# Thirty-two row scatters in front of 159 adding transfers on one GpSimd queue: eight ahead, the others one behind each of the first 24 adds

## The reference, cut to what matters

```python
tki = jax.lax.top_k(masked, TOPK)[1]                      # 8 of 32 experts for each token
...
combine = (jax.nn.one_hot(tki, E, dtype=tkw.dtype) * tkw[..., None]).sum(1)
g = jax.nn.silu(jnp.einsum('th,eih->tei', h, w_gate))
u = jnp.einsum('th,eih->tei', h, w_up)
routed = jnp.einsum('tei,ehi->th', g * u * combine[:, :, None], w_down)
...
return (routed + shared).reshape(B, S, Hd)
```

## Time and profile before

| | |
|---|---|
| median of 3 runs | 3811.11 us (3809.53 to 3814.87) |
| the profiled execution's own time | 3820.71 us |
| its span, first to last instruction | 3819.0 us |
| busy in the span: PE, DVE, ACT, POOL | 90%, 63%, 47%, 13% |
| stage G | from 3439 us to the end |
| 32 scatters of the last batch on POOL | 3439.1 to 3479.9 us |
| 159 adds on POOL | 3486.9 to 3783.0 us |

### The profile page before, as it was taken

How to read it: one execution, slowest core, us unless ns; L and a number is a source line. 1 busy time by engine, 2 the same in 40 slices (tenths; PEclk the granted TensorE clock), 3 DMA queues, 4 the chain that set the end, 5 groups by cost and what they waited for, 6 DMA issues and landing times.

```text
span 3819.0 us, 62855 instructions
## 1 busy us (share of the span) xinstructions
PE 3441.5 (90%) x21953; PEld 1664.1 (44%) x21953; DVE 2416.8 (63%) x6385; ACT 1804.2 (47%) x3597; POOL 511.0 (13%) x451
## 2 busy tenths in 40 slices
PE   6999989998999889998999899999999889997992
PEld 2352445344352445343452445343452445345881
DVE  5668576755668576854768576853768566853552
ACT  2755534452755434443846434443836434532551
POOL 0000020000001120000002120000002020007885
PEclk9999999999999999999999999999999999998996
DMA  6313001304314101314214101215213201937997
GB/s 215 117 36 69 20 2 49 50 22 152 104 40 94 40 6 49 46 59 148 84 36 91 37 11 48 42 59 174 68 37 84 102 18 47 259 145 170 163 162 171
DMA packets 184290, 317.61 MB, mean 83 GB/s; under 512 B 29972, under 2 KB 139412, under 8 KB 178580
## 3 DMA queue, kind: packets, MB, share of 16 engines
q1 hardware_dynamic: 152888, 270.90, 25.5%
q0 software_dynamic: 29040, 39.86, 5.9%
q10 hardware_dynamic: 2032, 2.61, 0.2%
HBM read 176.94 MB, written 116.70 MB: 77 GB/s over the span
## 4 chain that ended last, share of the span: by engine, by line
PE 70%; DVE 19%; ACT 4%; issue 3%; SPq 1%; DMA 1%; PEldq 1%; another core or an unknown queue 1%; POOL 0%; PEld 0%; POOLq 0%; DVEq 0%; ACTq 0%
PE ps L607 8%; PE ps L590 7%; PE ps L429 5%; DVE mx L773 5%; PE ps L534 4%; PE ps L1865 4%; PE ps L1472 4%; PE ps L1762 3%; PE ps L595 3%; PE ps L1803 3%; PE ps L486 2%; PE ps L1786 2%; DVE ps L770 2%; PE ps L1487 2%; PE ps L638 2%
## 5 line engine op out<-in xcount | busy, mean ns | idle before, releaser
L711 ACT ACTIVATE PT<-ps 128x512 f32<-128x512 f32 (+2 forms) x1280 | 643.9, 564 | 330.3 <-PE ps L595 174.6
L773 DVE TENSOR_REDUCE mx<-ps 128x1 f32<-128x512 f32 (+3 forms) x768 | 431.0, 618 | 84.8 <-PE ps L534 46.0
L590 PE MATMUL ps<-QS,KS 99*128 99x512 bf16 (+2 forms) x1280 | 420.2, 369 | 8.6 <-ACT PT L711 6.9
L534 PE MATMUL ps<-KS,QS 96*128 96x512 bf16 (+3 forms) x1280 | 395.2, 371 | 17.5 <-DVE mx L773 7.1
L770 DVE CUSTOM_DVE_ANT_0 ps<-ps,mneg 128x512 f32<-128x512 f32 x512 | 340.9, 718 | 82.0 <-PE ps L534 78.9
L607 PE MATMUL ps<-PT,VP 128*32 128x512 f32 (+3 forms) x2560 | 375.4, 576 | 0.0
L429 PE MATMUL ps<-mneg,identb 128*128 128x512 bf16 x1240 | 329.1, 394 | 29.3 <-DVE a_fin L1980 10.9
L407 POOL TENSOR_TENSOR rstd<-mv,half 128x4 f32<-128x4 f32 x20 | 20.3, 1015 | 2499.1 <-DVE mv L374 2499.1
L590 PEld LDWEIGHTS ps<-QS,KS 99*128 99x128 bf16 x1280 | 108.5, 97 | 394.0 <-ACT PT L711 234.1
L1452 POOL DMA_INDIRECT sums<-wbuf,ctxT x159 | 247.7, 1558 | 55.3 <-issue 36.9
L1980 DVE TENSOR_TENSOR a_fin<-a_fin,ps 128x512 f32<-128x512 f32 (+1 forms) x176 | 104.6, 635 | 209.9 <-PE ps L1845 208.5
(11 more groups left out here) (334 smaller groups left out, 6015.9 us busy)
## 6 DMA issues: line engine op xcount, KB each, us to landing
slot_rows<-in_padrows SPq DMA_DIRECT2D x32, 725.0 KB, 20.0
scores<-a_fin SPq DMA_DIRECT2D x64, 256.0 KB, 3.0
a_fin<-scores SPq DMA_DIRECT2D x32, 512.0 KB, 4.6
KS<-KP SPq DMA_DIRECT2D x240, 64.0 KB, 2.6
g_xb<-slot_rows SPq DMA_DIRECT2D x105, 145.0 KB
a_Y<-in_wA SPq DMA_DIRECT2D x4, 3072.0 KB, 13.5
scores<-a_fin SPq DMA_DIRECT2D x64, 192.0 KB, 3.0
a_fin<-scores SPq DMA_DIRECT2D x12, 1024.0 KB, 7.9
```

Of the source, the lines that this page charges most:

```text
L534: last = nc.tensor.matmul(o, m["QS"][0:KR, h, i * P:(i + 1) * P], m["KS"][0:KR, h, f:f + w], start=True, stop=not c.causal)
L590: last = nc.tensor.matmul(o, m["KS"][0:KST, h, j * P:(j + 1) * P], m["QS"][0:KST, h, q0:S], start=True, stop=plain)
L711: nc.scalar.activation(m["PT"][:, mp % 2, j % 2, e, 0:w], ps[:, SLOTS + n % TURNED, 0:w], ACT.Exp, scale=HD ** -0.5).then_inc(g("exp"), 1)
L773: nc.vector.tensor_reduce(m["mx"][:, h % 2, i, f // BANK:f // BANK + 1], ps[:, k % SLOTS, 0:w], AX.X, ALU.max, negate=True).then_inc(g("sl ...
```

## The change

`g_pool` no longer issues the 32 scatters in one go. SOON = 32 // 4 = 8 go first, and behind each of the adds of blocks 0 to 23 goes one of the other 24. Nothing else is altered.

```diff
         XSLOTS = NI * DM // ROW
+        SOON = NI * TOPK // 4
         LATE = (0, 1, 2, 3, 4, 19, 20)
...
         def g_pool(pool):
             g = lambda s: sm["G", s]
-            for k in range(NI * TOPK):
+            for k in range(SOON):
                 to_slot(k)
             pool.wait_ge(x_stored, 16)
             pool.wait_ge(zeroed, 16 * NACC)
...
                                              in_=MG["y"][:, b % RY, :], in_offset=None, compute_op=ALU.add).then_inc(g(f"added{b % NACC}"), 16)
+                if SOON + b < NI * TOPK:
+                    to_slot(SOON + b)
```

## The result

The changed kernel takes 3823.64 us (median of 7 runs, 3819.05 to 3827.84), the kernel before beside it 3811.11 us (7 runs, 3807.98 to 3814.87): a ratio of 1.0033, with a 95% interval of 1.0021 to 1.0045. It is slower by 12.5 us, with 8 to 17 us inside the interval. Timed once more, on a chip that the record calls chip 3, the ratio was 1.0030 (1.0019 to 1.0042); the chip of the first comparison is not on record.

What follows compares the result with a forecast made beforehand. POOL's chain of scatters and adds was taken to bound the last stage. 3811.1 us plus 12.7 us of new idle time, with the old taken as 0, gave 3823.8 us, range 3815 to 3834.

Steps and rivals of the forecast that it cites:

- The bound: In the last stage POOL's chain sets the end; from first add to last it waits for nobody, adds 1.864 us apart.
- The new idle time: POOL's wait in the changed kernel between the eighth scatter and the first add: 12.7 us, 15.4 at the late end.
- The old idle time: POOL's wait in the kernel before between last scatter and first add: 6.6 us profiled, taken as 0 without the profiler.
- stretching: SP's register operations at the densest scatters taking 0.705 and 0.709 us instead of 0.152 and 0.018, with late ACT instructions.
- rival 1: Timed runs of the kernel before have the stretching too and the change removes it: +6.1 us, 3817.2 us; chance 27%.
- Hidden costs named at nothing: Moved scatters beside DVE add nothing, upper bound 17.3 us; SP's wait before block 65 and PE's for buffers cost nothing.
- rival 3: PE, waiting for buffers, drops to 1.2 GHz: about nothing for 30 blocks, 3850 us or more if longer; chance 2%.
- Rival 2: The stretching stays in the changed kernel, POOL idles 37 us: +30.4 us, 3841; through the alternation 31 us more; chance 12%.

## Why the prediction was right

**The bound.** "From the first add to the last POOL waits for nobody" held, and with it that the 24 moved scatters are paid in full: 30.4 us by the sum, 30.7 us between the last stages with and without them.

**The new idle time.** 12.7 us forecast; 13.0 and 13.2 us measured in two profiles of the changed kernel. The step behind it (first add at 3462.6 to 3465.3 us on the old scale, 23.5 to 26.2 us behind the first scatter) held: 3454.92 - 3431.24 = 23.7 us behind the first scatter, the early end.

**The old idle time.** This was the open term, 0 or 6.6 us. I took 0, because the slow register operations looked like the price of recording. The timed +12.5 and +11.4 us agree with 0 in both comparisons of the changed kernel; 6.2 (ratio 1.0016) is outside both intervals. The reason that I gave is wrong: on chip 3 a recorded execution of 32 dense scatters has no stretching, and on chips 2 and 10 the unrecorded ones behave as if they had it. There the change would cost an estimated 386.9 - 380.7 = 6.2 us; it was not timed on them. So the mechanism of the forecast (new idle time less old) held, but that the old idle time was 0 was in part luck: it hangs on the chip or session of the comparison, and the 27% for rival 1 were better than they looked.

**Hidden costs named at nothing.** The scatters beside DVE cost 0.02 us each, so the earlier trace rows was the right row for them. The rule of the Trainium skill ("SBUF — State Buffer", section "Who interferes with whom"), that a DVE instruction in a two-port mode and GpSimd block each other for the whole instruction, is not tested here, since no row names the mode of an instruction. DVE's longest was of 0.48 us, and no scatter of the alternation took over 0.99 us. SP loads block 65 at 3551.24 us in the changed kernel's profile, 21.6 us behind the start of the last scatter, so none landed too late. PE was stopped by full result buffers and nothing came of it, and its clock stayed high, so rival 3 fell. Rival 2 (stretching through the alternation) fell too: both profiles of the changed kernel are free of it, though they come from the group where nothing else is stretched. On chips 2 and 10 the kernels with eight first have their first add 23.9 and 24.0 us behind the first scatter, and the pairs of the kernel with none first pass every 3.15 us, so that neither eight scatters nor the alternation brings a delay there.

**What stays open.** What makes the stretching. Of six profiles with 18 or more dense scatters five have it, while the scatters last, and the sixth is from chip 3; with eight or none no first result is late. Right behind the eight of the second run with 24 left out single instructions of SP are slow all the same, up to 0.671 us:

```profile
L1431 SPq SEQ_ASSERT  x3: 18/406/671, 3444.9 to 3448.7; - x3
```

It thus needs dense scatters and something else that differs between chips or sessions. Which of the two it is no run shows, since each of the three chips has one session on record. Nor was the kernel before ever profiled in the group where it takes 3810 us: that it is free of the stretching there is argued from the times, from the mark above and from the kernel with 32 first and no adds.

## What to carry to other kernels

An engine with 13% of the span can be the only one that counts in the last 10% of it: look at the end of the chain, and divide the stretch between first and last instruction by their number. On such an engine reordering gains only if it fills idle time, and putting work that is ready behind work that isn't makes idle time: let it do what is ready until the first result comes, here at least 18 of the 32 scatters (timed only on chips 2 and 10). Compare single profiles from a common event inside the changed stage, since the unchanged 3430 us ahead of it varied by 8 us, more than the 6.4 us between the two profiled stages. And where two groups of chips or sessions give different times, put a profile beside times of its own group only.

## What the runs showed of the hardware

In the profiles of chips 2 and 10 and in that of the kernel before, register operations and asserts of SP took 0.7 us each, some 1.4, beside 18 or more dense indirect scatters of GpSimd, instead of 0.018 and 0.152. ACT stood idle for up to 10.22 us ahead of an instruction meanwhile, but no instruction of its sequencer is on record as slow, so what held it is not shown. POOL's own pitch stayed at 1.265 us, and PE was through with block 1 as early as without it. The first result came 24 us later with 32 scatters (first add 48.5 us behind the store instead of 24.5) and 8 and 6 us later with 18, in the two profiles. In the same profiles a 0.037 us operation of SP took up to 0.41 us beside the adds, and POOL's adds passed all the same at their usual pitch. On chip 3 neither was there.
